# Cross-attention L0X of a decoder: heads in pairs, probabilities turned by transposing DMAs, query rounding on Pool

## The reference, cut to what matters

```python
q = (x @ Wq + bq).reshape(1, B * N, H, hd)          # 2048 rows, 16 heads of 16
kv = (cond @ Wkv + bkv).reshape(1, -1, 2, H, hd)    # 8 * 64 = 512 keys for every row
k, v = (kv[:, :, 0], kv[:, :, 1])
q = jnp.transpose(q * scale, (0, 2, 1, 3))          # k and v likewise, without scale
q = _fq_sym(q, axis=-1); k = _fq_sym(k, axis=-1); v = _fq_sym(v, axis=2)
attn = softmax(einsum('bhqd,bhkd->bhqk', q, k), axis=-1)
attn = _fq_unsigned(attn, axis=-1)
out = einsum('bhqk,bhkd->bhqd', attn, v)            # heads side by side: 256 features
x = _layernorm(x + out @ Wp + bp)

def _fq_sym(x, axis):        # _fq_unsigned: max(x) / 255, clip 0 to 255
    s = maximum(max(abs(x), axis) / 127.0, 1e-8)
    return clip(round(x / s), -127, 127) * s
```

## Time and profile before

| | |
|---|---|
| median of the runs | 4113.47 us |
| profiled execution, its own time | 4110.44 us |
| its span, first to last instruction | 4108.4 us |
| PE, PEld, DVE, ACT, POOL busy | 81%, 59%, 68%, 48%, 10% |
| DMA queue of the program | 46.57 MB, 2.9% of 16 engines' span |
| L0X set-up block | 274.5 to 320.3 us |
| L0X loop block | 322.7 to 761.5 us |
| L0X closing block | 764.1 to 774.2 us |
| next sublayer's first instructions | 776.8 us |

### The profile page before, as it was taken

One profiled execution on the slowest core, in us unless ns is written; L12 is line 12 of the kernel. 1 busy time (PEld: TensorE's weight loads), 2 busy tenths in 40 slices (PEclk: granted clock), 3 DMA queues, 4 the chain that ended last, 5 costly groups with the idle time before them and its releaser, 6 DMA issues. The chain is left out here.

```text
span 4108.4 us, 59566 instructions
## 1 busy us (share of the span) xinstructions
PE 3335.9 (81%) x18333; PEld 2417.8 (59%) x18364; DVE 2798.4 (68%) x8822; ACT 1969.4 (48%) x5854; POOL 407.3 (10%) x495
## 2 busy tenths in 40 slices
PE   7967888697999999674569976559999999999565
PEld 5644545474777777463237764227777777777344
DVE  4667888537788887566964437866666666666597
ACT  4537888414555555123521112336666666666243
POOL 0000000001111110110111100001111111111100
PEclk9986666799999999876569988569999999999588
DMA  1000000100000000000000012000000000000000
GB/s 55 2 23 1 1 1 1 80 1 13 1 1 1 1 1 1 39 1 29 1 15 1 1 43 100 1 11 1 1 1 1 1 1 1 1 1 1 32 1 21
DMA packets 6585, 50.37 MB, mean 12 GB/s; under 512 B 256, under 2 KB 4480, under 8 KB 4608
## 3 DMA queue, kind: packets, MB, share of 16 engines
q1 hardware_dynamic: 6272, 46.57, 2.9%
HBM read 44.47 MB, written 2.10 MB: 11 GB/s over the span
## 5 line engine op out<-in xcount | busy, mean ns | idle before, releaser
L2162 DVE CUSTOM_DVE_ANT_0 L3A_masked<-ps,L3A_hidden,L3A_negrstd 128x128 f32<-128x128 f32 (+1 forms) x512 | 193.5, 415 | 324.7 <-PE ps L2053 235.0
L2111 ACT ACTIVATE L3A_probs<-L3A_masked,L3A_negmax 128x128 f32<-128x128 f32 (+1 forms) x512 | 228.6, 449 | 238.2 <-DVE L3A_negmax L2162 238.2
L331 PE MATMUL ps<-s_weights_b,s_XT 128*128 128x512 f32 (+1 forms) x648 | 302.5, 596 | 24.7 <-ACT L1A_qn L1969 9.1
L2081 PE MATMUL ps<-s_weights_b,L3A_OT 128*128 128x256 f32 x1024 | 265.7, 382 | 14.8 <-DVE s_R L2191 14.8
L331 PE MATMUL ps<-s_weights_b,s_Xc 128*128 128x512 f32 x512 | 244.2, 599 | 7.8 <-DVE L3A_rot L2026 3.3
L877 ACT ACTIVATE L0X_pf<-ps,L0X_negmax_scaled,L0X_qscale 128x512 f32<-128x512 f32 x256 | 209.4, 818 | 54.8 <-DVE L0X_negmax_scaled L923 53.5
L2034 POOL TENSOR_TENSOR L3A_rstd<-L3A_ve,s_mhalf 128x4 f32<-128x4 f32 x144 | 145.1, 1008 | 854.4 <-DVE L3A_ve L1994 854.4
L918 DVE TENSOR_REDUCE L0X_negmax<-ps 128x1 f32<-128x512 f32 x256 | 176.4, 689 | 55.4 <-PE ps L816 47.3
L2081 PEld LDWEIGHTS ps<-s_weights_b,L3A_OT 128*128 128x128 f32 x1024 | 175.7, 192 | 29.2 <-issue 15.9
L868 ACT ACTIVATE L0X_pT<-ps,L0X_less 128x512 bf16<-128x512 f16 x256 | 184.9, 723 | 9.7 <-PE ps L825 9.6
L331 PEld LDWEIGHTS ps<-s_weights_b,s_XT 128*128 128x128 f32 x648 | 124.4, 211 | 109.0 <-issue 68.1
(11 more groups left out here) (512 smaller groups left out, 9038.7 us busy)
## 6 DMA issues: line engine op xcount, KB each, us to landing
s_weights_b<-w_L3A SPq DMA_DIRECT2D x1, 9984.0 KB, 27.0
s_weights_b<-w_L1A SPq DMA_DIRECT2D x1, 7936.0 KB, 21.3
s_weights_a<-w_L2F SPq DMA_DIRECT2D x1, 4224.0 KB, 13.9
s_weights_b<-w_L1F SPq DMA_DIRECT2D x1, 3840.0 KB, 13.1
s_weights_b<-w_L3F SPq DMA_DIRECT2D x1, 3136.0 KB, 10.4
...
```

What stands on the lines that cost most here:

```text
L331: last = pe.matmul(out, lhs(k), rhs(k), start=(k == 0), stop=(k == n - 1))
L2081: last = pe.matmul(c.bank(3)[:, j * DM:(j + 1) * DM], OT[:, u % 4, j * P:(j + 1) * P], w["wo"][:, h, :], start=(h == 0 and j == 0), stop=( ...
L2111: last = a.activation(pr[:, u % 4, cols], ms[:, u % 2, cols], ACT.Exp, bias=nmx[:, h, j:j + 1], scale=-1.0, accum_out=sm[:, h, j:j + 1])
L2162: last = eng.tensor_tensor_reduce(out=ms[:, u % 2, cols], in0=s[:, cols], in1=hidden[:, P - j * P:2 * P], scale=-1.0 if gated else nrs[:, ...
```

## The change

L0X becomes one block. A unit is a pair of heads, of which there are 128; slots s run from 0 to 143, and in each PE writes the scores of pair s and the value products of pair s-6, DVE takes the maxima of both heads in one operation and rounds pair s-2 in one operation, and ACT does two exps. The factor 255 goes into the exp as a bias of log 255, so the rounding is an addition and a subtraction in one operation that gives bf16. The transposes on PE, their copy out of PSUM by ACT and the fp16 identity are no longer used: SP issues one transposing DMA for a pair (128 x 1024 bf16, SBUF to SBUF), with four buffers ph and pT. The scores take banks 0 to 5, the outputs bank 6, and all side work of a sequence goes through bank 7 in six steps (X, Q, T0, T1 for the sequence after at slots 0, 1, 6, 7 of 16; oT, Y for the one before at slots 9, 10); each step waits on PE until the step before has left the bank. The queries' division, rounding and three casts move from DVE to POOL (pool_q), and so do the three-part splits of the keys; the value scales are multiplied into the rows of wp, so that VS and its products go; x + bp is made on POOL. The closing block goes: the last sequence's steps are in slots 128 to 143.

```diff
+    PAIRS = TT * HEADS // 2
+    U = SEQS * PAIRS
+    SLOTS = range(U + PAIRS)
+    LN255 = float(np.log(255.0))
+    VALUE_LAG = 6
+    STEP_AT = {0: ("X", 1), 1: ("Q", 1), 6: ("T0", 1), 7: ("T1", 1), 9: ("oT", -1), 10: ("Y", -1)}
...
+        kx = c.oT
...
+        pf = S.sb("pf", [P, 3, 2, KEYS])
+        ph = S.sb("ph", [P, 4, 2, KEYS], BF16)
+        pT = S.sb("pT", [P, 4, 2, KEYS], BF16)
...
+        def pe_side(pe, x):
+            what, i = x
+            m = number[x]
+            if m:
+                pe.wait_ge(side_act, act_through(steps[m - 1]))
+                pe.wait_ge(side_vec, vec_through(steps[m - 1]))
...
+        def vec_side(v, x):
+            what, i = x
+            if what not in BY_VEC:
+                return
+            e = v.eng
+            e.wait_ge(side_made, number[x] + 1)
+            if what == "Q":
+                if i:
+                    e.wait_ge(q_parts, TT * i)
+                v(e.tensor_tensor(row[:], halves, over(w["bq"], TT), ALU.add), side_vec)
+                v(e.tensor_reduce(am[:], heads_of(flat(row[:]), 2 * HEADS), AX.X, ALU.max, apply_absolute_value=True))
+                v(e.tensor_scalar(qs[:, i % 2, :], am[:], DH ** -0.5 / 127.0, 1e-8, ALU.mult, ALU.max))
+                v(e.reciprocal(inv[:], qs[:, i % 2, :]))
+                v(e.tensor_scalar(inv[:], inv[:], DH ** -0.5, None, ALU.mult), q_scaled)
+            else:
+                e.wait_ge(xb_ready, i + 1)
+                v(e.tensor_tensor(c.R[:], Xb[:], halves, ALU.add), side_vec)
...
+        def pool_q(p, i):
+            g = p.eng
+            g.wait_ge(q_scaled, i + 1)
+            if i:
+                g.wait_ge(side_made, number["T1", i - 1] + 1)
+            else:
+                g.wait_ge(k_turned, KT)
+            p(g.tensor_tensor(heads_of(flat(tmp[:]), 2 * HEADS), heads_of(flat(row[:]), 2 * HEADS), spread(inv[:], DH), ALU.mult))
+            p(g.tensor_scalar(tmp[:], tmp[:], MAGIC, MAGIC, ALU.add, ALU.subtract))
+            for j in range(TT):
+                for part in range(3):
+                    p(g.tensor_copy(parts(j)[:, part], heads_of(tmp[:, j, :])), q_parts if part == 2 else None, free=True)
...
+                for p in range(U):
+                    sp.wait_ge(steps_ready, p + 1)
+                    if p >= 4:
+                        sp.wait_ge(o_made, p - 3)
+                    sp.dma_start_transpose(out=pT[:, p % 4].rearrange("p x (t q) -> p (x t) q", q=P), in_=flat(ph[:, p % 4])).then_inc(
+                        turned[p % 4], 16)
...
+                def scores(p):
+                    b, j, m = place(p)
+                    if p == 0:
+                        pe.wait_ge(kT_ready, KT)
+                        pe.wait_ge(v_ready, KT)
+                    if p % PAIRS == 0:
+                        pe.wait_ge(side_act, act_through(("T1", b)))
+                    if p >= 3:
+                        pe.wait_ge(exp_ready, p - 2)
+                    for x in range(2):
+                        r = slice(ROWS * x, ROWS * x + ROWS)
+                        last = pe.matmul(c.bank(2 * (p % 3) + x), qT[r, b % 2, m, j * P:(j + 1) * P], kT[r, m, :], start=True, stop=True)
+                    last.then_inc(scores_made, 1)
+
+                def values(p):
+                    b, j, m = place(p)
+                    pe.wait_ge(turned[p % 4], 16 * (p // 4 + 1))
+                    if b and p % PAIRS == 0:
+                        pe.wait_ge(o_read, b)
+                    for x in range(2):
+                        h = 2 * m + x
+                        for t in range(KT):
+                            last = pe.matmul(c.bank(6)[:, j * DM + h * DH:j * DM + (h + 1) * DH], pT[:, p % 4, x, t * P:(t + 1) * P],
+                                             V[:, t, h * DH:(h + 1) * DH], start=(t == 0), stop=(t == KT - 1))
+                    last.then_inc(o_made, 1)
+
                 pe.wait_ge(S.loaded, 16)
...
+                for x in steps[:2]:
+                    pe_side(pe, x)
...
+                for s in SLOTS:
+                    if s < U:
+                        scores(s)
+                    if s in step_at:
+                        pe_side(pe, step_at[s])
+                    if 0 <= s - VALUE_LAG < U:
+                        values(s - VALUE_LAG)
...
+                def exps(p):
+                    b, j, m = place(p)
+                    a.wait_ge(max_ready, p + 1)
+                    if p >= 3:
+                        a.wait_ge(steps_ready, p - 2)
+                    for x in range(2):
+                        at = j * HEADS + 2 * m + x
+                        last = a.activation(pf[:, p % 3, x, :], c.bank(2 * (p % 3) + x), ACT.Exp, scale=qs[:, b % 2, at:at + 1],
+                                            bias=nms[:, p % 4, x:x + 1], accum_out=sm[:, b % 2, at:at + 1])
+                    last.then_inc(exp_ready, 1)
+
...
+                def maxima(p):
+                    b, j, m = place(p)
+                    eng.wait_ge(scores_made, p + 1)
+                    v(eng.tensor_reduce(nmx[:, p % 4, :], c.ps[:, 2 * (p % 3):2 * (p % 3) + 2, :], AX.X, ALU.max, negate=True))
+                    for x in range(2):
+                        at = j * HEADS + 2 * m + x
+                        v(eng.tensor_scalar(nms[:, p % 4, x:x + 1], nmx[:, p % 4, x:x + 1], qs[:, b % 2, at:at + 1], LN255,
+                                            ALU.mult, ALU.add), max_ready if x else None, free=True)
+
+                def steps_of(p):
+                    eng.wait_ge(exp_ready, p + 1)
+                    if p >= 4:
+                        eng.wait_ge(turned[p % 4], 16 * (p // 4))
+                    v(eng.tensor_scalar(ph[:, p % 4], pf[:, p % 3], MAGIC, MAGIC, ALU.add, ALU.subtract), steps_ready, free=True)
...
+                for s in SLOTS:
+                    if s < U:
+                        maxima(s)
+                    if 0 <= s - 2 < U:
+                        steps_of(s - 2)
+                    if s in step_at:
+                        vec_side(v, step_at[s])
+                    i = s // PAIRS - 1
+                    if i >= 0 and s % PAIRS == VALUE_LAG - 1:
+                        outputs(i)
+                    if i >= 0 and s % PAIRS == 13:
+                        S.vec_norm_scale(v, i + 1, i)
+
...
+                    g.wait_ge(k_rows, t + 1)
                     if t >= 2:
-                        eng.wait_ge(turned, t - 1)
+                        g.wait_ge(k_turned, t - 1)
...
+                            p(g.tensor_tensor(heads_of(x), heads_of(x), o, ALU.subtract))
+                    g.sem_inc(k_parts, 1)
...
-                def turn(u):
-                    pe.wait_ge(steps_ready, u + 1)
-                    if u >= 2:
-                        pe.wait_ge(probs_ready, u - 1)
-                    o = c.bank(6 + u % 2, F16)
-                    for t in range(KT):
-                        last = pe.transpose(o[:, t * P:(t + 1) * P], ph[:, u % 2, t * P:(t + 1) * P], c.idh[:])
-                    last.then_inc(probs_turned, 1)
...
-                def take(u):
-                    a.wait_ge(probs_turned, u + 1)
-                    if u >= 3:
-                        a.wait_ge(o_made, u - 2)
-                    a.activation(pT[:, u % 3, :], c.bank(6 + u % 2, F16)[:, 0:KEYS], ACT.Identity,
-                                 bias=less[:, 0:1]).then_inc(probs_ready, 1)
...
-                    eng.tensor_scalar(ph[:, u % 2, :], pf[:, u % 3, :], 255.0, HALF_MAGIC, ALU.mult,
-                                      ALU.add).then_inc(steps_ready, 1)
...
-        S.last_rows(w["wp"], w["bp"])
```

More of the change, by code:

```diff
@@ L642, in sublayer_l0_cross, with act_through, vec_through @@
     QCH = HEADS * ROWS // P
+    PAIRS = TT * HEADS // 2
[4 more added lines that the diff above has]
+    STEP_AT = {0: ("X", 1), 1: ("Q", 1), 6: ("T0", 1), 7: ("T1", 1), 9: ("oT", -1), 10: ("Y", -1)}
+    steps = [("X", 0), ("Q", 0), ("T0", 0), ("T1", 0)]
+    step_at = {}
+    for s in SLOTS:
+        if s % PAIRS in STEP_AT:
+            what, ahead = STEP_AT[s % PAIRS]
+            i = s // PAIRS + ahead
+            if 0 <= i < SEQS:
+                step_at[s] = (what, i)
+                steps.append((what, i))
+    number = {x: m for m, x in enumerate(steps)}
+    BY_ACT, BY_VEC = ("X", "T0", "T1", "oT"), ("Q", "Y")
+    def act_through(x):
+        return sum(y[0] in BY_ACT for y in steps[:number[x] + 1])
+    def vec_through(x):
+        return sum(y[0] in BY_VEC for y in steps[:number[x] + 1])
     with Sublayer(core, n) as S:
@@ L693, in vec_q_quantize, with place @@
-        def vec_q_quantize(v, j, b):
-            quantize_heads(v, row[:, j, :], am[:], qs[:, b, j, :], inv[:], tmp[:])
-        def vec_q_parts(v, j):
-            for part in range(3):
-                v(v.eng.tensor_copy(parts(j)[:, part], heads_of(tmp[:])), q_ready if part == 2 else None, free=part < 2)
-        def pe_turn_q(pe, j, t=0):
-            pe.wait_ge(q_ready, TT * t + j + 1)
```

(48 more changed lines are left out.)

295 lines of the change are left out of this document (106 added, 189 removed).

## The result

The changed kernel takes 4043.58 us (median of four, 4040.17 to 4047.47) against 4114.82 us (median of four): a ratio of 0.9827, interval 0.981 to 0.9844. The forecast was 4038, its range 3972 to 4108. The profiled execution took 4040.17 us with a span of 4038.4, 70.0 less than the span before.

A forecast was written before the change was run, and what follows sets the result against it. ACT's copy out of PSUM bounded the steady loop, with DVE 17% below. Gains of 49.5 (loop), 22 (set-up) and 4 us (tail), 75.5 off 4110.4, gave 4035, or 4038 as a median; range 3972 to 4108.

The forecast's parts named there:

- The loop: First maximum to end of last: from 430.5 us to 381, at 47.6 us for each of eight sequences.
- the mechanism that was named: In the loop, DVE becomes the limit and idles three times a sequence while side steps on PE hold the next scores.
- The waits behind Q, T1 and Y: DVE's idle times in a loop sequence: 2.7, 2.3 and 2.7 us at the lower clock; 7.2 taken in all.
- the first rival: Side steps cost the loop nothing, DVE alone limits at 40.4 us a sequence; kernel 3980 us; chance 0.14.
- The DMA: A pair's transposing DMA in the loop needs less than 2.9 us of the queue and hides behind DVE.
- the bounds of 0.6 and 4.9: Microseconds a pair for the transposing DMA: 0.6 from the slope of long loads, 4.9 if none overlaps another.
- POOL: Its query operations between Q and T0 in the loop: 4.3 us a sequence within 9 us, costed at nothing.
- The set-up: DVE's first operation to first maximum: 46.7 us before, first maximum near 301, 22 us earlier, bounds 17 to 25.
- The tail: End of last maximum to next sublayer: 18.4 us instead of 23.0, with 3 for the DMA; gain taken as 4.

The follow-up runs named there:

- The spread kernels: Two: the changed kernel with its side steps moved apart, 3997.10 us; and that with X also made a sequence earlier, 3980.74 us.
- the full queue: The changed kernel with every pair transposed twice, the first copy into a spare area: 4052.71 us, DMA engines at a share of 0.96.

## Why the prediction was right, step by step

The loop: right, 380.9 for 381, and by the mechanism that was named, though the exact hit is luck. The limit moved from ACT to DVE, whose work with its small gaps came to 40.3 us a sequence where 40.4 had been forecast. The waits behind Q, T1 and Y were 3.4, 1.7 and 3.3 us, where 2.7, 2.3 and 2.7 had been worked out: 8.4 where 7.2 had been taken. But only seven sequences have them in the loop, since the last one prepares no queries and its own Y stands in the tail. So they cost 58.6 us, and the forecast had 8 x 7.2 = 57.6: two errors that cancel. The spread kernels show both halves: take the waits away and 319.5 us remain, near the first rival's 323. That rival lost because PE does not get ahead across a step, as argued.

One wait had not been seen. PE's products of the first pair of a sequence wait for the outputs of the one before (24.4 us behind s_On in seven sequences). DVE takes its next maximum 0.1 us behind those outputs, so it did not idle for it.

The DMA: hidden, as taken. Landing takes 3.1 us and the queue can do a pair in 1.5, between the bounds of 0.6 and 4.9. Of the two statements of the Trainium skill the trace is nearer to "Advanced Engine Details and Errata" (X-Bar Transpose (TRN2)), yet its 350 to 400 GB/s is twice what the full queue moved, 171 GB/s. The 1309 ns a block in "VectorE: DVE Perf Modes" (The three transpose paths) can't be a price of throughput: eight blocks landed in 3.1 us.

POOL: its query operations took 5.7 us a sequence where 4.3 had been priced, and PE never waited for them in the loop, so costing them at nothing was right.

The set-up: the gain was 18.9 us instead of 22, and the step that failed is two waits taken at nothing. A key tile cost POOL the 2.9 us that had been forecast, but POOL waited 1.3 us before the third tile, because PE turned the first one only behind the first query projection. And behind the fourth tile POOL waited 2.1 us for PE to turn it, because the query parts are written to the same buffer. Together that is about what the first maximum came late, 27.8 us behind DVE's first operation where the terms gave 24.3:

```profile
287.04 0.40 POOL L960 CAST L0X_rq<-s_oT 128x256 bf16<-128x256 f32 x1 [1.33 <-PE ps L699]
...
292.76 0.40 POOL L960 CAST L0X_rq<-s_oT 128x256 bf16<-128x256 f32 x1
...
295.24 1.06 POOL L776 TENSOR_TENSOR L0X_tmp<-L0X_row,L0X_inv 128x512 f32<-128x512 f32 x1 [2.08 <-PE ps L699]
```

A price was wrong too, but cost little. POOL's two-step rounding was priced at 0.61 from the row of a plain copy and took 1.93. PE could begin T0 when half of the casts were done, though, so from POOL's product to T0 (299.62) were 4.4 us, where 4.3 had been taken:

```profile
296.39 1.93 POOL L777 TENSOR_SCALAR L0X_tmp<-L0X_tmp 128x512 f32<-128x512 f32 x1
```

On DVE key tiles came every 3.3 us rather than 2.66, since POOL's operations stretch DVE's; POOL's fourth tile did not wait for them. Two roundings of a key tile (256 columns), the first with POOL still waiting, the second beside it:

```profile
278.64 0.29 DVE L626 TENSOR_SCALAR L0X_tmp<-L0X_tmp 128x256 f32<-128x256 f32 x1
...
281.23 0.76 POOL L962 TENSOR_TENSOR s_oT<-s_oT,L0X_rq 128x256 f32<-128x256 f32 x1
...
281.50 0.65 DVE L626 TENSOR_SCALAR L0X_tmp<-L0X_tmp 128x256 f32<-128x256 f32 x1
```

The page "SBUF — State Buffer" of the Trainium skill (Who interferes with whom) says that one instruction holds the shared ports to its end. The trace agrees for POOL's operations on two tensors: 0.65 for 0.29 here, 1.48 for 0.68 in the loop, each ending behind POOL's. It does not for POOL's two-step rounding: the DVE rounding at 506.47 took 0.83 and ended 0.8 us before POOL's, as far as POOL's recorded spans can be trusted. Over the loop the stretching came to 6 us (128 roundings, 0.733 on average for 0.684), where the prediction's estimate by that page was 10.

The tail: wrong in size, 23.3 instead of 18.4. Two terms failed. The last transfer landed late: the last rounding ended at 688.27 us, and its products started at 694.01, 5.7 us where 3 had been taken. Three roundings follow each other at the end, and for 0.9 us of this SP was still issuing the transposes before; the last one then took 4.8 us to land, the longest of all 128, and why is open.

```profile
687.58 0.69 DVE L902 TENSOR_SCALAR L0X_ph<-L0X_pf 128x1024 bf16<-128x1024 f32 x1 [0.49 <-ACT L0X_pf L862]
...
694.01 0.38 PE L817 MATMUL ps<-L0X_V,L0X_pT 128*128 128x16 bf16 x8 [2.46 <-DMA L0X_pT<-L0X_ph]
```

And from the last norm (704.10 + 0.86) to the next sublayer (708.84) are 3.9 us where 2.6 had been taken. These two make 4.0 of the 4.9. In the profiled executions the gain was 70.0 us where 75.5 had been forecast: 0.1 more in the loop, 3.1 less in the set-up, 4.3 less in the tail, 1.8 more elsewhere.
